# GNN kernel on one core: the five last phases rebuilt around pairs of tiles, with the dst-row batch-norm scale left on GpSimd

## What is computed

```python
x = layernorm(x + L0(x))   # edge MLP, sum over dst, node MLP
# L1: out = agg @ W_l + b_l + x @ W_r ; batch norm over all rows ; leaky relu ; + x
x = layernorm(x + L1(x))
# L2: per-edge products of node features with filters, summed over src, small node MLP
x = layernorm(x + L2(x))
# L3: q, k, v = x @ W ; per-edge attention over src (max, exp, weighted sum), out = sum / denom
x = layernorm(x + L3(x))
```

## Time and profile before

| | us |
|---|---|
| median of 3 runs | 2497.8 (2497.32 to 2498.23) |
| the profiled execution | 2496.8 |
| its span | 2495.1 |
| busy: PE, DVE, POOL, ACT | 1919.1, 1518.4, 1434.5, 955.9 |
| the five last phases, from 1550.7 | 944.4 |
| mean granted PE clock, share of full | 0.861 |

### The profile page before, as it was taken

The page is one execution under the profiler, slowest core; times in us unless marked ns, Lnnn a source line. Parts: engine busy times, 40 slices in busy tenths (PEclk is TensorE's granted clock), DMA queues, the critical chain, the costliest instruction groups (busy, mean ns, idle before and its releaser), DMA issues. The chain is left out here.

```text
span 2495.1 us, 25120 instructions
## 1 busy us (share of the span) xinstructions
PE 1919.1 (77%) x5516; PEld 946.9 (38%) x5516; DVE 1518.4 (61%) x2662; ACT 955.9 (38%) x1608; POOL 1434.5 (57%) x1773
## 2 busy tenths in 40 slices
PE   5999995999999999999997910334578788857700
PEld 3444442444444444444443400223355433323300
DVE  5464451777777777777771606866377577755544
ACT  2344342555555555555552302222356322212211
POOL 2211111666656666566665324887677488877866
PEclk9999997999999999999998955555587899978855
DMA  7732124344444444444445433232433233335632
GB/s 260 246 114 47 17 30 120 134 155 147 165 144 158 152 150 160 142 165 149 153 144 176 88 47 106 64 66 59 136 119 110 85 127 127 127 105 138 144 102 98
DMA packets 176741, 310.26 MB, mean 124 GB/s; under 512 B 33809, under 2 KB 47026, under 8 KB 176406
## 3 DMA queue, kind: packets, MB, share of 16 engines
q1 hardware_dynamic: 143558, 233.66, 27.3%
q0 software_dynamic: 29760, 71.21, 13.0%
q10 hardware_dynamic: 3344, 4.51, 0.6%
HBM read 169.54 MB, written 139.76 MB: 124 GB/s over the span
## 5 line engine op out<-in xcount | busy, mean ns | idle before, releaser
L657 PE MATMUL d_p_h<-w3a,d_xT 128*128 128x512 f32 x640 | 289.6, 596 | 26.1 <-DMA d_xT<-in_xT 26.1
L657 PE MATMUL d_p_o<-d_w,d_uT 128*128 128x512 f32 x640 | 288.1, 593 | 3.0 <-ACT d_uT L732 3.0
L657 PE MATMUL d_p_p<-d_wr,d_x1T 128*128 128x512 f32 x640 | 289.4, 595 | 0.0
L548 POOL TENSOR_SCALAR d_small<-d_mv 128x1 f32<-128x1 f32 x160 | 82.0, 512 | 300.4 <-DVE d_mv L783 150.7
L814 DVE TENSOR_TENSOR d_zz<-d_yg,d_xbeta 128x512 f32<-128x512 f32 x80 | 138.6, 1732 | 99.0 <-POOL d_yg L865 99.0
L657 PEld LDWEIGHTS d_p_h<-w3a,d_xT 128*128 128x128 f32 x640 | 122.3, 191 | 180.6 <-issue 180.6
L657 PEld LDWEIGHTS d_p_o<-d_w,d_uT 128*128 128x128 f32 x640 | 121.3, 190 | 155.7 <-issue 151.2
L657 PEld LDWEIGHTS d_p_p<-d_wr,d_x1T 128*128 128x128 f32 x640 | 116.0, 191 | 116.4 <-issue 116.4
L725 ACT ACTIVATE d_yn<-d_y,d_small 128x512 f32<-128x512 f32 x80 | 65.0, 813 | 228.4 <-POOL d_small L553 228.4
L280 PE MATMUL m_p_H<-m_xT,m_w 128*128 128x512 f32 x320 | 147.7, 616 | 4.8 <-ACT m_xT L321 4.8
L1153 ACT ACTIVATE plain_y<-plain_y,plain_small 128x512 f32<-128x512 f32 x80 | 64.8, 810 | 206.8 <-POOL plain_small L553 206.8
(11 more groups left out here) (248 smaller groups left out, 4521.9 us busy)
## 6 DMA issues: line engine op xcount, KB each, us to landing
sum<-d_zeros SPq DMA_DIRECT2D x80, 260.0 KB, 2.1
sum<-m_tile_sum SPq DMA_DIRECT2D x10, 2048.0 KB, 7.8
d_xT<-in_xT SPq DMA_DIRECT2D x80, 256.0 KB, 2.6
d_z<-sum SPq DMA_DIRECT2D x80, 256.0 KB, 2.9
d_x<-in_x SPq DMA_DIRECT2D x80, 256.0 KB, 3.1
x<-d_x SPq DMA_DIRECT2D x80, 256.0 KB
p<-d_p SPq DMA_DIRECT2D x80, 256.0 KB, 2.0
plain_p<-p SPq DMA_DIRECT2D x80, 256.0 KB, 2.8
```

Source lines behind the costliest of these rows:

```text
L548: nc.gpsimd.tensor_scalar(tmp, var, factor, add, ALU.mult, ALU.add).then_inc(done, 1)
L657: last = nc.tensor.matmul(out[:, :], lhsT[:, c, :], w[:, c, :], start=(c == 0), stop=(c == KB - 1))
```

## The change

It rewrites the five last phases.

- **Layer norm factor.** `row_scale` on POOL is replaced in these phases by `reciprocal_deviation` on ACT: a logarithm, an exponential, and a product with the negated mean for each of two tiles. DVE negates the mean (one more small operation for two tiles).
- **Pairs.** Plain tiles are handled two at a time: 40 pairs of [128, 2, 512], loads and stores of 512 KB, two buffers. Shift, leaky relu and residual work on 1024 columns at once. 10 pairs are in the equivariant phase, 14 in scores, 16 in values, spread evenly over the steps by `spread_over`. The batch-norm scale and the shift of the pairs are DVE's.
- **Edge rows.** Shift and leaky relu work on the dst and src rows of a tile at once; the message comes one step behind instead of three, the scatter two behind instead of five; the src gather goes ahead of the dst gather. The scale of the dst rows stays a POOL multiplication.
- **Attended rows.** Two tiles at a time; POOL only gathers and scatters.

```diff
-PLAIN_BUFS = 4
+PAIRS = NODE_TILES // 2
+PAIRS_Q, PAIRS_S, PAIRS_V = 10, 14, 16
...
+def reciprocal_deviation(nc, k, act, var, neg_mean, rstd, shift, done, base, norms=1):
+    n = var.shape[-1]
+    col = 0 if norms == 1 else 1
+    nc.scalar.activation(rstd, var, ACT.Ln, bias=k.eps[:, col:col + 1], scale=norm_factors(norms)[0]).then_inc(done, 1)
+    act.wait_ge(done, base + 1)
+    nc.scalar.activation(rstd, rstd, ACT.Exp, scale=-0.5).then_inc(done, 1)
+    act.wait_ge(done, base + 2)
+    for i in range(n):
+        nc.scalar.activation(shift[:, i:i + 1], neg_mean[:, i:i + 1], ACT.Copy, scale=rstd[:, i:i + 1]).then_inc(done, 1)
...
+def spread_over(steps, n):
+    return [(i * n) // steps != ((i + 1) * n) // steps for i in range(steps)]
...
+def pair_load(nc, k, sp, j):
+    b, rows = j % 2, slice(j * 2 * P, (j + 1) * 2 * P)
+    if j >= 2:
+        sp.wait_ge(k.pair_y, j - 1)
+    sp.dma_start(k.pair_p[b][:, :, :], k.p[rows, :].rearrange("(p a) d -> p a d", a=2)).then_inc(k.pair_p_in[b], 16)
+    sp.dma_start(k.pair_x1[b][:, :, :], k.x1[rows, :].rearrange("(p a) d -> p a d", a=2)).then_inc(k.pair_x1_in[b], 16)
...
+def pair_leaky(nc, k, dve, j):
+    dve.wait_ge(k.pair_p_in[b], 16 * (j // 2 + 1))
+    nc.vector.tensor_tensor(a, a, wide(k.bn_scale), ALU.mult).then_inc(k.pair_scaled, 1)
+    dve.wait_ge(k.pair_scaled, j + 1)
+    nc.vector.tensor_tensor(a, a, wide(k.bn_shift), ALU.add).then_inc(k.pair_shifted, 1)
+    dve.wait_ge(k.pair_shifted, j + 1)
+    nc.vector.scalar_tensor_tensor(out=a, in0=a, scalar=0.01, in1=a, op0=ALU.mult, op1=ALU.max
+                                   ).then_inc(k.pair_leaky, 1)
...
 edge_rows_phase, gpsimd:
+            def scale(t):
+                if t >= 2:
+                    pool.wait_ge(y_done, 2 * t - 2)
+                nc.gpsimd.tensor_tensor(a[t % 2][:, 0, :], rows_of(2 * t), k.bn_scale[:, :], ALU.mult
+                                        ).then_inc(dst_scaled, 1)
...
-                if 1 <= t <= T:
-                    row(2 * t - 2)
-                    row(2 * t - 1)
                 if t + 1 < T:
-                    scale(2 * t + 2)
-                if 0 <= t - 5 < T:
-                    scatter(t - 5)
+                    scale(t + 1)
                 if t + 2 < T:
+                    gather(2 * t + 5)
                     gather(2 * t + 4)
-                    gather(2 * t + 5)
+                if 0 <= t - 2 < T:
+                    scatter(t - 2)
...
 attended_rows_phase, gpsimd:
+            for g in range(BUFS):
+                gather(g)
+            for g in range(G):
+                scatter(g)
+                if g + BUFS < G:
+                    gather(g + BUFS)
```

More of the change, by code:

```diff
@@ L1082, in plain_transfers @@
[L1082 to L1095, removed]
@@ L1127, in plain_moments @@
[L1127 to L1144, removed]
-        pool.wait_ge(k.plain_out, i - PLAIN_BUFS + 1)
-    row_scale(pool, k, mv[:, 1:2], mv[:, 0:1], small[:, 0:1], small[:, 1:2], small[:, 2:3], k.plain_sc, 3 * i,
-              norms=3)
@@ L1150, in plain_row, with tail_buffers @@
[L1150 to L1154 removed]
+def tail_buffers(nc, k):
+    k.tail = ExitStack()
+    sb = lambda name, shape: k.tail.enter_context(nc.sbuf_tensor("pair_" + name, shape, F32, side="right"))
+    sem = lambda name: k.tail.enter_context(nc.semaphore("pair_" + name))
+    two = lambda name, shape: [sb(f"{name}{i}", shape) for i in range(2)]
+    k.pair_p, k.pair_x1, k.pair_rows = (two(n, [P, 2, D]) for n in ("p", "x1", "rows"))
+    k.pair_stats, k.pair_mv = two("stats", [P, 2, 6]), two("mv", [P, 2, 2])
+    k.pair_neg, k.pair_rstd, k.pair_shift = (two(n, [P, 2]) for n in ("neg", "rstd", "shift"))
+    k.eps = sb("eps", [P, 2])
+    k.eps_set = sem("eps_set")
+    k.pair_p_in, k.pair_x1_in, k.pair_gone = (
+        [sem(f"{n}{i}") for i in range(2)] for n in ("p_in", "x1_in", "gone"))
+    k.pair_scaled, k.pair_shifted, k.pair_leaky, k.pair_y, k.pair_st, k.pair_moments, k.pair_ready, k.pair_sc, k.pair_out = (
+        sem(n) for n in ("scaled", "shifted", "leaky", "y", "st", "moments", "ready", "sc", "out"))
@@ new lines, in pair_transfers @@
+def pair_transfers(nc, k, sp, first, end):
+    for j in range(first, end):
+        pair_load(nc, k, sp, j)
+        if j >= 2:
+            pair_store(nc, k, sp, j - 2)
+def pair_leaky(nc, k, dve, j):
+    b = j % 2
+    a = k.pair_p[b][:, :, :]
+    wide = lambda row: row[:, :].rearrange("p (a d) -> p a d", a=1).to_broadcast([P, 2, D])
+    dve.wait_ge(k.pair_p_in[b], 16 * (j // 2 + 1))
[5 more added lines that the diff above has]
+                                   ).then_inc(k.pair_leaky, 1)
@@ L1157, in edge_rows_phase, with pair_normalise @@
+def pair_normalise(nc, k, act, j):
+    b = j % 2
+    act.wait_ge(k.pair_ready, j + 1)
+    reciprocal_deviation(nc, k, act, k.pair_mv[b][:, :, 1], k.pair_neg[b], k.pair_rstd[b][:, :], k.pair_shift[b],
+                         k.pair_sc, 4 * j, norms=3)
+    for s in range(2):
+        row = k.pair_rows[b][:, s, :]
+        nc.scalar.activation(row, row, ACT.Identity, bias=k.pair_shift[b][:, s:s + 1],
+                             scale=k.pair_rstd[b][:, s:s + 1]).then_inc(k.pair_out, 1)
 def edge_rows_phase(nc, k):
+    tail_buffers(nc, k)
@@ L1410, in _ @@
         def _(pool):
-            def gather(u):
+            for u in range(U):
                 if u >= AHEAD:
```

458 lines of the change are left out of this document (212 added, 246 removed).

## The result

The changed kernel takes 2429.2 us (median of 4 runs, 2428.45 to 2436.68) against 2497.6; the ratio is 0.9733 with a 95% interval of 0.9714 to 0.9753. Forecast were 2425 us, a range of 2390 to 2452, and faster with a chance of 0.93. The five terms of the sum, −73, stand against 944.4 − 877.6 = −66.8 in the windows. The profiled execution of the change took 2436.7, 7 us above the median: its unchanged first three phases ended 6.8 us later than in the trace before (the edge rows begin at 1557.5, not at 1550.7).

What follows compares the result with a forecast made beforehand. POOL's small work was taken to set three phases, no engine bounding any throughout. Terms of −25 (edge rows), −7 (equivariant), −31 (scores), −2 (values) and −8 (attended rows) make −73 on 2496.8; adjusted to the median, 2425 us, range 2390 to 2452.

Steps and rivals of the forecast that it cites:

- stated signs of being wrong: DVE idling for gathers in the edge rows, a scores step without a pair over 10 us, or a longer values phase.
- Edge rows, −25 forecast: Edge rows phase: 12 us to the first moments, 19 steps of 8.25, 22 at the end; 191 us for 216.
- I take 1.25: Edge rows: POOL's remaining multiplication holds DVE up 1.25 us a step (bounds 0 and 1.27), making DVE's 7.0 into 8.25.
- The first rival: Edge rows: POOL's left-over multiplication runs beside the moments and costs nothing; 7.0 us a step, 2401 us in all; chance 0.20.
- Equivariant, −7 forecast: Equivariant phase: 4.15 us a unit for 4.31, mixed from DVE's 3.9 and PE's 5; 5 us, and 2 more at the end.
- Scores, −31 forecast: Scores phase: 13 steps of 11.9 us with a pair and 6 of 7.7 without make 201; −35, with 4 given back.
- The 4 us given back for the chain of the maximum: Scores phase: 4 us lost because the maximum's gather waits for the previous step's scatter on a path through DVE.
- Values, −2 forecast: Values phase: scatters, each waiting for the one before, set 6.7 us a step for 6.79; bounds −8 and +15.
- I take 6.7: Values phase: step time chosen from 6.3 to 6.8 us, a scatter's 5.8 to landing plus 0.5 to 1.0 until the next.
- The second rival: Values phase turns to loads and stores: every step costs a pair's 7.7 us, 19 us more, 2444 in all; chance 0.18.
- Attended rows, −8 forecast: Attended rows phase: two tiles take 3.57 and 4.8 us, 8.3 a pair; 76 us from first to last scatter for 83.7.
- The rival on the slower side: Scores phase: PE falls to the lower clock, 19.6 us a step, +187 us, 2612 in all; chance 0.05.

## Why the prediction was right, and where its steps were off

**The total** came out 4 us from the forecast, and that nearness is partly luck. Against the windows the five terms are off by +9.2, −4.4, −4.1, +8.3 and −2.8 us, in the order of the phases, and these errors cancel down to 6.2. All five lie within their own bounds. One of the stated signs of being wrong did come: the values phase is longer than before (163.0 us against 156.7), so for that phase the account failed. The other two did not: DVE waits for a gather in the edge rows only once, at the start (5.2 us), and the steps without a pair in the scores phase take 6.1 (the first 7.9).

**That POOL's small work was the price:** right, as far as it was tried. The edge rows and the attended rows put back give their windows back (14 of 15.8 and 10 of 10.8 us), and the scale of the pairs put back into POOL's list in the scores phase costs 59 us of the 68 gained. How the 35 us of the scores phase divide between the row scales, the pairs and the moved multiplications was not taken apart, nor was the equivariant phase.

**Edge rows, −25 forecast, −15.8 measured.** Three of the four parts hold: 12 to the first moments (11.7), 22 from the last moments to the end (22.7), and DVE's own step 7.0 (6.98 with the multiplication cut away). The term that was mis-sized is the stop by the multiplication, "I take 1.25", bounded by 1.27 from above: it is 1.75 (8.73 − 6.98). 19 × 0.48 is 9 us, all by which this phase's term was off. The bound was the multiplication's own length, and that length is right: 1.26 us with free neighbours. What the bound left out is where the multiplication stands in the new order, directly behind the issue of a scatter. There DVE is held before the multiplication's own 1.27 begin: the shift for 1.72 us and the negation for 2.48. In the kernel before, the scatter came after it.

The mean of the group before would have been a poor guide too:

```profile
L1210 POOL TENSOR_TENSOR e_a<-dst_rows_sb,bn_scale 128x512 f32<-128x512 f32 x20 | 29.9, 1498 | 0.0
```

Its 1498 ns are above 1.27 because in ten steps DVE came first and POOL was the one that waited (start, duration, engine, line):

```profile
1619.27 0.69 DVE L1252 TENSOR_TENSOR e_a<-e_other,bn_scale 128x512 f32<-128x512 f32 x1 [1.36 <-DMA e_other<-p,index]
1619.37 1.72 POOL L1210 TENSOR_TENSOR e_a<-dst_rows_sb,bn_scale 128x512 f32<-128x512 f32 x1
```

DVE's operation keeps its 0.69 us and POOL's takes 1.72, 0.45 more than alone. In the earlier trace rows it is the other way round: POOL came first and kept its 1.27, and DVE took 1.59. The rule of the Trainium skill ("SBUF — State Buffer", Who interferes with whom) that was cited there fits these rows for the two-operand work, and with the multiplication beside one-operand moments the price is 0 (6.97 a step). The negation, which reads one operand, was stopped as well; the rule as it was cited does not cover that.

**The first rival, that the multiplication costs nothing (0.20),** did not happen, but it is what a wait of one line brings about: 2396.8, where 2401 had been worked out for it. Its argument against, that the start drifts in POOL's list, is the right one: in the change 7 of 20 multiplications catch the negation in full and 8 the shift.

**Equivariant, −7 forecast, −11.4 by the windows (−10.5 with the border set right).** From the addition of unit 0 to the last it was 153.9 us and is 144.4. The first 32 units took 4.07 each (4.31 before) where 4.15 had been mixed from DVE's pace and PE's, so 3 of the missing us are there. The granted clock of the window rose from 0.72 to 0.76, which fits fewer units at PE's slower pace; neither that nor why it rose was tried.

**Scores, −31 forecast, −35 measured.** The steps came to 201.4 us against 201 worked out, and PE's limit of 9.8 was met exactly in two runs. The 4 us given back for the chain of the maximum were too much: without them the term is −35, and no wait of DVE for that chain shows. Single steps alternate 13.45, 11.7 and 6.1 us, so the assumed pair of 11.9 and 7.7 was right only in sum.

**Values, −2 forecast, +6.3 measured.** The step that failed is "I take 6.7" a step, with the chain of scatters as the limit and DVE's work hidden under it; it is 7.02 (6.8 to 7.0 in nine other traces of the same code), and DVE is the limit in most steps. I had worked out DVE's limit as 7.65 for a step with a pair and then let the scatter chain decide, with DVE's 126 us in all below it. The two do not overlap like that: a step with a pair takes 7.39, near enough to 7.65, and the fifteen of them between first and last, with four short steps of 0.7, would be 114 us. The other 19 are DVE's three waits for a gather behind the scatters (4.88 + 6.33 + 5.69) and one of 2.2 for a store: two of the four steps without a pair, the sixth and the eleventh, still take 7.2 and 6.6 us, because DVE then waits for a gather that stands in POOL's list behind scatters that have not landed. The larger of the two limits counts in each step, not the larger of the sums. With a pair in each step those waits are gone, and 19 steps take 140.2. The second rival's 7.7 in every step was too much, since loads and DVE overlap: DVE waits for no load of a pair in this phase. Its direction was right, though the cause is DVE's work and not the transfers.

**Attended rows, −8 forecast, −10.8 measured:** 73.4 us for 76. A scatter with two gathers behind it takes 3.83 us to the next one, where 4.8 was taken, and the other 3.91 instead of 3.57: 7.7 a pair for 8.3. A gather's issue was put at the 1.35 of the rows before; it is 0.97 here.

The rival on the slower side did not come: the clock in the scores phase went from 0.90 to 0.93.

## What to carry to other kernels

When work stays on POOL beside a busy DVE, ask not only how long it takes but what DVE runs at that moment: here 1.26 us of multiplication cost 1.75 a step beside the shift or the negation and nothing beside the moments, and one wait decided which. To size such a stop, look in each record at which engine came first, since here only the later one was longer, and at what stands in front of the work in its own list; neither the shortest member nor the mean of the group says that. And where two limits are near each other, add up the larger one step by step; the larger of the two sums is too low.

## What was not expected of the hardware

- Where POOL's multiplication and a two-operand operation of DVE meet, only the later one is longer: DVE's 0.69 beside POOL's 1.72 when DVE began 0.10 us earlier, and 1.59 beside 1.27 when POOL did.
- Behind the issue of a scatter the multiplication is recorded with 1.85 to 1.88 us in place of 1.27, of which 0.55 overlap that issue, and DVE is held in this overlap as well.
- The negation, an operation on two columns with one operand, was stopped for 2.65 us seven times. Each time it began 0.3 us after POOL had begun to issue the scatter and 0.75 before the recorded start of the multiplication, and ended with the multiplication. Where only the scatter's issue met it, in the run with the scale on DVE, it took 0.22. Why an issue with a multiplication behind it holds DVE, and one without does not, was not tried.
- A scatter with add of the values phase lands 4.9 us after its issue without pair transfers beside it, 6.4 with 16 pairs, and 5.0 with 20 pairs at an even pace. More traffic did not make it slower there; why is open.
